# Decoder layers on one core: the dense experts' matmuls read the weight table with a step of 32 bytes

## The reference

```python
logits = jnp.clip(xt @ gate_w.T, -50.0, 50.0)
top_w, top_idx = jax.lax.top_k(logits, 2)
rw = jax.nn.softmax(top_w, axis=-1)
deltas = jax.nn.softmax(expert_atom_weights, axis=-1) @ atoms
weighted = deltas * jax.nn.sigmoid(importance) 
rows = mask_idx // H
cols = mask_idx % H
vals = jnp.einsum('tk,tks->ts', rw, weighted[top_idx])
contrib = jax.ops.segment_sum((xt[:, cols] * vals).T, rows, num_segments=H)
out = xt @ W.T + contrib.T
```

## Time and profile before

| | |
|---|---|
| Time, median of 3 runs | 487.9 us (483.1 to 489.0) |
| The profiled execution | 483.95 us, of which the span of the trace is 482.2 |
| TensorE busy | 382.3 us (79%) |
| VectorE busy | 306.0 us (63%) |
| ScalarE busy | 216.5 us (45%) |
| GpSimd busy | 116.0 us (24%) |
| Stage 3, dense part | about 103.7 to 137.4 us of the span |

### The profile page before, as it was taken

One profiled execution on the slowest core, in us unless ns is written; L12 is line 12 of the kernel. 1 busy time (PEld: TensorE's weight loads), 2 busy tenths in 40 slices (PEclk: granted clock), 3 DMA queues, 4 the chain that ended last, 5 costly groups with the idle time before them and its releaser, 6 DMA issues.

```text
span 482.2 us, 6927 instructions
## 1 busy us (share of the span) xinstructions
PE 382.3 (79%) x2443; PEld 224.8 (47%) x2443; DVE 306.0 (63%) x615; ACT 216.5 (45%) x546; POOL 116.0 (24%) x215
## 2 busy tenths in 40 slices
PE   5997935859879799999872877776764798999993
PEld 2564524624335367566551233433332543665562
DVE  2988655767962687878728897687984273122234
ACT  3641401373014766765313798779996412010000
POOL 7233778775042000000052111111111000000002
PEclk9979975859999899999987598799897699999997
DMA  8990111400000000000000399999997503211211
GB/s 294 273 350 13 3 2 2 175 0 1 0 0 1 0 3 1 1 2 1 2 0 1 65 204 185 181 155 175 215 138 129 175 1 81 82 45 44 65 44 44
DMA packets 68993, 38.01 MB, mean 79 GB/s; under 512 B 56864, under 2 KB 63968, under 8 KB 68512
## 3 DMA queue, kind: packets, MB, share of 16 engines
q1 hardware_dynamic: 66656, 37.52, 33.3%
q0 software_dynamic: 2304, 0.07, 1.3%
HBM read 21.58 MB, written 2.88 MB: 51 GB/s over the span
## 4 chain that ended last, share of the span: by engine, by line
PE 52%; DVE 14%; DMA 11%; ACT 10%; POOL 7%; issue 5%; POOLq 0%; SPq 0%; ACTq 0%; DVEq 0%
PE ps L760 25%; ACT area_b L690 7%; DMA area_a<-area_b 7%; PE ps L1162 6%; PE ps L945 5%; PE ps L956 5%; POOL deltas L492 4%; DMA area_b<-area_b 3%; PE ps L975 3%; PE ps L939 2%; DMA deltas<-entry_w,small 1%; POOL rstd L463 1%; DVE res L1362 1%; DVE res L1364 1%; DVE stats L1274 1%
## 5 line engine op out<-in xcount | busy, mean ns | idle before, releaser
L1526 DVE CUSTOM_DVE_ANT_0 area_a<-ps,zero,small 128x1024 f32<-128x1024 f32 x64 | 79.4, 1279 | 15.2 <-ACT area_b L690 11.6
L690 ACT ACTIVATE area_b<-area_a,small 128x1024 int16<-128x1024 f32 x64 | 72.8, 1139 | 11.3 <-DMA area_a<-area_b 7.6
L671 ACT ACTIVATE area_a<-ps,small 128x256 f32<-128x256 f32 (+1 forms) x128 | 51.8, 434 | 29.7 <-DVE small L1417 28.7
L462 POOL TENSOR_SCALAR var_eps<-meanvar 128x1 f32<-128x1 f32 x24 | 7.9, 330 | 232.8 <-DVE meanvar L1275 232.6
L760 PE MATMUL ps<-xT_odd,area_a 128*128 128x512 f32 x128 | 57.3, 594 | 0.0
L1054 PE MATMUL ps<-area_b 128*128 128x512 bf16 x128 | 44.0, 437 | 14.8 <-DVE small L1526 13.9
L1584 DVE TENSOR_TENSOR area_b<-ps,area_b 128x512 f32<-128x512 f32 x16 | 11.1, 691 | 51.9 <-ACT area_b L735 51.9
L1417 DVE TENSOR_REDUCE small<-ps 128x4 f32<-128x1024 f32 (+1 forms) x24 | 29.3, 1223 | 16.9 <-PE ps L945 16.6
L735 ACT ACTIVATE area_b<-ps 128x512 f32<-128x512 f32 x16 | 9.5, 596 | 63.4 <-PE ps L760 63.4
L760 PEld LDWEIGHTS ps<-xT_odd,area_a 128*128 128x128 f32 x128 | 24.1, 190 | 25.7 <-issue 25.2
L760 PE MATMUL ps<-area_b,xT_even 128*128 128x512 f32 x64 | 31.1, 637 | 4.9 <-ACT area_b L648 3.2
(11 more groups left out here) (267 smaller groups left out, 668.8 us busy)
## 6 DMA issues: line engine op xcount, KB each, us to landing
area_a<-in_w_up_dram SPq DMA_DIRECT2D x8, 512.0 KB, 4.4
area_b<-gates_out SPq DMA_DIRECT2D x16, 256.0 KB, 3.0
deltas<-area_b SPq DMA_DIRECT2D x1, 2112.0 KB, 16.2
area_b<-deltas SPq DMA_DIRECT2D x2, 1024.0 KB, 5.8
area_a<-in_w_down_dram SPq DMA_DIRECT2D x1, 2048.0 KB, 8.8
area_b<-in_idx_row_dram SPq DMA_DIRECT2D x1, 1024.0 KB, 7.5
ctxT<-in_ctxT_dram SPq DMA_DIRECT2D x1, 1024.0 KB, 10.1
ctx_tok<-in_ctx_dram SPq DMA_DIRECT2D x1, 1024.0 KB, 18.6
```

The lines of the kernel that those rows point to most:

```text
L671: a = act.activation(p1[:, n % 2, x * nk * P:(x + 1) * nk * P], scores1(n)[:, x * nk * P:(x + 1) * nk * P], ACT.Exp, bias=nmx1[:, n % 2, x ...
L690: act.activation(px[:, u % PX, :], sx[:, u % 3, :], ACT.Exp, bias=nbx[:, u:u + 1], accum_out=zx[:, i, h:h + 1]).then_inc(sem("px_ready"), 1)
L1526: dve.tensor_tensor_reduce(sx[:, u % 3, :], bank(2 * (u % 2), 2), zero[:].broadcast_to([P, B * M]), qsc[:, i, h:h + 1], LOWEST, ALU.add, A ...
```

## The change

The eight copies on ScalarE are removed, and `delta` with them. TensorE waits for the two read-back DMAs itself and takes the moving operand out of `raw`: two experts of 256 columns each, with a step of eight f32 values from column to column. Order and number of the matmuls, their results and what uses them stay.

```diff
@@ -180,7 +180,6 @@
         raw = carve("b", 4 * NS, [DC, D * E0])
-        delta = carve("b", 2 * NS, [DC, E0, D])
@@ -642,12 +641,6 @@
                 for k in range(EARLY):
                     take_kTx(k)
-                for pair in range(E0 // 2):
-                    for c in range(DC):
-                        act.wait_ge(sem(f"deltas_{c}"), 16)
-                        act.activation(delta[:, c, 2 * pair:2 * pair + 2, :],
-                                       raw[:, c, :].rearrange("p (r e) -> p e r", e=E0)[:, 2 * pair:2 * pair + 2, :],
-                                       ACT.Copy).then_inc(sem("delta_ready"), 1)
                 for k in range(EARLY, KT):
                     take_kTx(k)
@@ -904,14 +897,15 @@
                 pe.wait_ge(sem("kx_out"), KT)
+                for c in range(DC):
+                    pe.wait_ge(sem(f"deltas_{c}"), 16)
                 for y in range(TT * E0 // 2):
                     i, pair = divmod(y, E0 // 2)
-                    pe.wait_ge(sem("delta_ready"), DC * min(y + 1, E0 // 2))
                     if y >= 4:
 
                         pe.wait_ge(sem("y_used"), y - 3)
                     dense(bank(y % 4), tile_of(2, i),
-                          lambda c: delta[:, c, 2 * pair:2 * pair + 2, :].rearrange("p e r -> p (e r)")).then_inc(sem("y_ps"), 1)
+                          lambda c: raw[:, c, :].rearrange("p (r e) -> p e r", e=E0)[:, 2 * pair:2 * pair + 2, :]).then_inc(sem("y_ps"), 1)
```

## The result

The changed kernel took 509.1 us (median of 5 runs, 503.8 to 510.8) against 487.9 us (483.1 to 489.0, 5 runs); the ratio is 1.0448, 95% interval 1.0386 to 1.0511. The profiled execution took 503.8 us, with a span of 502.0. The forecast was 505 us in a range of 480 to 513, with 503.6 for the profiled execution. Executions of one kernel come faster and slower by some microseconds: in this text medians are over all runs, while the ratios with their intervals compare the faster runs alone, so that the two can differ by up to 0.8%.

The account below looks back on a forecast made before the run. VectorE was taken to bound the stage, TensorE just ahead; strided records (54.8 us), key turns (2.0) and tail (0.2) from 100.5 us, plus the last pair, added 19.7 us to 483.95, giving 503.6; 505 was said, range 480 to 513.

Parts of the forecast that it names:

- 0.55 us a record: Dense matmuls of stage 3: VectorE hides TensorE up to this pace; beyond it each 0.1 us costs 6.4 us.
- first wait: Before the first dense matmul: TensorE no longer waits for ScalarE's copies, so the stage starts 3.2 us earlier.
- six other copies: ScalarE copies running beside matmuls in stage 3: nothing waited for them after the first four results, so removal gains zero.
- 64 x 0.857 = 54.8: Dense matmuls of stage 3: 64 records at 0.857 us each take 54.8 us with the strided operand.
- twice the present fast pace: Each strided dense record on TensorE takes 0.857 us instead of 0.429 us, chosen from ScalarE's copy of the same pattern.
- likeliest case: Dense records on TensorE double to 0.857 us: 505 us, own range 499 to 513, chance 0.64.
- at the low clock nothing more is lost: Dense records at the low clock: their pace there is already that of the strided reads, 0.857 to 0.91 us.
- A (no cost): Dense records: the step costs TensorE nothing, only the 3.2 us at the start count; 480.8 us, chance 0.18.
- One column a cycle: TensorE matmuls: the Trainium skill has throughput depend on column count alone, which would give rival A's time, 480.8 us.
- B (each pass fetches for itself): Dense records on TensorE: 1.71 us each, +74 us, 558 us in all; chance 0.10.
- C (a partial loss): Dense records: 0.55 to 0.80 us each as only some fetches stall; from A's time up to 500 us; chance 0.08.
- forecast of 19.7 us: End of stage 3: the last VectorE pair ends at 158.6 instead of 138.93, adding 19.7 us to the whole time.

Follow-up runs that it names:

- ladder of steps: Changed kernel, dense matmuls reading the table at steps of 1, 2, 3, 4 and 16 values: 483.2, 482.6, 493.9, 508.7 and 506.8 us.
- step 1: Changed kernel, but each dense matmul reads 512 neighbouring f32 values of the table: median 483.2 us, ratio 0.987 to the kernel before.
- pairs of kernels above: Wait kept against removed: kernel before against changed kernel reading neighbouring values (0.987); kernel before with only the 32-byte step (1.0531) against changed kernel (1.0448).
- early planes: Kernel before, with the first expert pair's copies moved ahead of the fourth turned key tile's eviction: median 482.8 us, ratio 0.9943.
- bf16: Changed kernel, both dense matmul operands read as upper bf16 halves of the f32 values, 32-byte step kept: median 482.9 us, ratio 0.9993.

## Why the prediction was right

**What bounds the stage.** The prediction had VectorE as the bound before the change, with TensorE just ahead of it (its last records end at 137.60, the last pair at 138.93) and room for TensorE up to 0.55 us a record, and TensorE as the bound after it. The ladder of steps bears that out: 0.45 us a record left the stage as it was with step 1 (36.3 against 36.1 us). The 0.55 was the point at which the changed kernel would be level with the one before: at 0.67 its stage is 48.4 - 39.5 = 8.9 us longer than before, where 64 x 0.12 = 7.7 us were to be expected.

**The copies.** Only the first wait was priced, 3.2 us; the stage shows 3.4 and 3.5 in the pairs of kernels above. The six other copies were worth nothing, as foreseen: the gain is the same with early planes, which keep all eight.

**The step.** The direction, the independence of the clock, and the reading of ScalarE's copy as the price of the pattern were right. The term that was mis-sized is "64 x 0.857 = 54.8": a record takes 0.918 us, so 58.8. That is 3.9 us and nearly the whole difference between the 59.2 us forecast for the stage (158.6 - 99.4) and the 62.95 measured. The failed choice was to take "twice the present fast pace" when the row it leaned on gave 1.77 ns a value, 0.91 us a record; ScalarE's rate was not merely near half, it was the very price. The likeliest case's own range, 499 to 513, took that rate in. That at the low clock nothing more is lost was wrong by a little: a record takes 0.92 us there too, where it took 0.86.

**The rivals.** A (no cost) was wrong in its condition, but its saving was right for a kernel without the step: 3.2 us forecast, 3.4 in the stage, and 2.2 between the medians (485.4 and 483.2). One column a cycle, which the prediction names beside it, isn't the pace of these f32 records even in a row: 0.429 us for 512 columns are two periods of 2.4 GHz a column. B (each pass fetches for itself) falls: 0.92 us and not 1.71; with bf16, one record for a matmul in place of two, a record costs as much as one of f32. C (a partial loss) exists, but only at a step of three values.

**From stage to time.** +23.5 us in the stage and +21.2 us in the median; the forecast of 19.7 us came nearer to the latter than its working earned, by the spread of the untouched part. That the profiled execution was met within 0.2 us (503.6 and 503.8) is luck: the stage came out 3.8 us longer than forecast, and the parts ahead of it and behind it, which the change doesn't touch, happened to be 0.8 and 2.9 us shorter.

## What to carry to other kernels

A moving operand of TensorE whose f32 values lay 4, 8 or 16 apart cost 1.7 to 1.8 ns a column, at least twice as much as in a row at a granted clock of 1.00, and TensorE was shown as busy all the time; look at the duration of a record or the distance of its weight loads. Here ScalarE's copy of the same pattern had the price beforehand: where another engine's row reads the pattern, take its rate as it is. An operand that is read 4 times, as here by four token tiles, is worth one sorting copy on an engine that has time, and the wait for it is better removed by making the first copy earlier (stages of 36.0 and 63.0 us).

## What was not expected of the hardware

Above its unstepped pace each step cost ScalarE and TensorE the same within 0.02 us for 512 values, and the order 8, 4, 16 from dear to cheap (1123, 1106, 1058 ns on ScalarE; 0.92, 0.90, 0.86 us on TensorE) is the same on both.

In the bf16 stage with the 32-byte step the granted clock was 0.50 throughout, though TensorE counted as busy for 34.58 of 34.84 us. In f32 with the same step and the same distance of records it rose within the stage (0.70 on average from 99.50 to 107.00, and 1.00 from there on). The engine is busy alike in both by the profile; the kernels differ in the type of the operands, and with it in the number of records (32 and 64). Which of these holds the clock down stays open. The low clock cost these records nothing, since their pace is the fetch's at either level.
